# Masking moved from TensorE to GpSimd, set-up waits split, and a new written order in a one-core two-layer kernel

## The chip, the cores and the metric

The kernel runs on one core of one Trainium2 chip. Five engines each run their own instruction stream, in order, and meet only at semaphores: TensorE (PE; its weight loads are listed as PEld), VectorE (DVE), ScalarE (ACT), GpSimd (POOL) and SyncE (SP), which issues nearly all DMAs. The metric is the time of the device in microseconds. The kernel before took 343.66 us (median of 3 runs, 339.81 to 346.64).

## The reference, cut to what matters

There are two sequences (B = 2) of 512 rows of 128 features. Three stages follow each other:

```
x = x + ffn0(softmax-scaled x)            # ternary weights, rounded activations: gate, up, down (128 -> 512 -> 128)
c = causal_attention(x, image)            # 16 heads of width 8; key 0 is one image key, keys 1.. are words
                                          # scores = where(kj <= qi + 1, q.k / sqrt(8), -10000) + mask; softmax; @ v; project
y = layernorm(c + full_attention(c))      # 16 heads again, no mask
y = layernorm(y + experts(y))             # 8 experts 128 -> 256 -> 128, one chosen per row
x = x + y
```

The products of queries and keys must be exact to float32, so each is held as three bfloat16 parts that are stacked along the contraction.

## The kernel before, in words

**Instances.** There are four attentions, `a` = 0 to 3: 0 and 1 are the causal one of either sequence, 2 and 3 the full one. Each has 64 `scores` steps (16 heads by 4 tiles of 128 queries; TensorE L1308 into a PSUM bank, VectorE takes the row maximum, L1025 for a < 2 and L1029 for a >= 2) and 32 `attend` steps. An `attend` step works on one head and two blocks of 128 keys: TensorE recomputes the scores turned round with the maximum already taken off (L1331), ScalarE takes the exponent into `probs` (L800, float32), and `values` steps multiply by the values (L1349). Four heads share one accumulation in `ps_pv`.

**The causal mask.** For a < 2 the blocks to the right of the diagonal are not computed. In the 128x128 block on the diagonal a future key has to count nothing: after each L1331 a second matmul (L1334) adds a triangle of -1e30 (`causal_k` by `identb`) before the exponent. There are 2 for each of 64 `attend` steps, 128 in all. The row maximum has its own triangle, added by L1025 on VectorE; the change leaves that alone.

**Set-up and the first stage.** SP loads all inputs (L478 to L508) and then copies zeroed rows three times (L511, 1 MB each). ScalarE sums the absolute weights (L689), scales them (L699); VectorE rounds weights (`ternary`, L842/L843) and x (`rounded_x`, L833/L836). For sequence a: `ffn_in` turns the rounded x; `ffn_up` (four tiles) is two matmuls (L1244), a Silu (L740), a product (L959) and a maximum (L962) on VectorE, and after the fourth tile a chain of small VectorE steps that ends in `q2_ready` (L972). `r2t` scales on ScalarE (L747, `Y`), rounds on VectorE (L976, `R2`) and turns on TensorE (L1253); `down` copies that from PSUM on VectorE (L979, `R2T`) and multiplies (L1262). `x1` adds the residual on VectorE (L986); `x1t` turns it (L1270), ScalarE copies (L755). `q` and `k` are one matmul each (L1284, L1288), ScalarE writes them in float32 (L763, L769) and then the high bfloat16 part (L766, L772). Steps `q_parts` and `k_parts` on VectorE make the rest (L993, L1000), the middle part (L994, L1001, a cast) and the low part (L996, L1003). `send` on SP writes the parts to DRAM (L544, L550) and loads them back stacked (L472); `scores` of that instance wait for these loads, and those of instance 0 also for `fixed_rows`, 12 small DMAs on SP (L521 to L526). `turn_weights` (TensorE L1195 to L1202, ScalarE L715 to L732), `prepare` (VectorE L928 to L943 with a small TensorE step, L1206 to L1209) and `images` (TensorE L1214 to L1228, ScalarE L751, VectorE L948 to L954) are set-up that the later stages need. The memsets of `Vs` (GpSimd, L624) come in the steps `stacks`.

**The order.** No planner runs in the kernel. The string `MERGE` is a written-out order: each letter takes the next step of a chain, every engine walks the same list and issues its own part of each step. So a step that stands earlier in the list on an engine holds up all that stands behind it there. In the old list the start reads, by steps: setup, ffn_in.0, turn_down, round_x, ffn_up.0[0-2], ffn_in.1, ffn_up.0[3], turn_weights, ffn_up.1[0], the r2t and down steps of sequence 0, prepare, x1.0, ffn_up.1[1-2], x1t.0, ffn_up.1[3], q.0, q_parts.0, k.0, k_parts.0, images, the r2t and down steps of sequence 1, scores.0[0-4], x1.1, scores.0[5-8], fixed_rows, more scores.0, send.0. The second instance's q_parts stands behind scores.0[49], its k_parts behind scores.0[53], and the first attend step behind scores.0[51].

**The end.** The experts (`hidden` L1424, `y` L1437, both TensorE in float32) follow the last attention; then a layer norm with small VectorE and GpSimd steps, and the output DMAs.

## Time and profile before

| what | value |
|---|---|
| runs of the kernel before | 343.66 us median of 3 (339.81 to 346.64) |
| the profiled execution, its own time | 341.08 us |
| its span, first to last instruction | 339.3 us |
| TensorE, matmul records | 294.3 us, 87% |
| VectorE | 256.6 us, 76% |
| ScalarE | 170.0 us, 50% |
| GpSimd | 28.6 us, 8% |
| mean granted TensorE clock | 0.943 |

A matmul's record runs from its start to its modelled end, and the next one may start long before that; so TensorE's busy time is an upper bound of the time for which it can take no further matmul. Two starts in a row tell what a matmul takes of the stream. The chain of waits follows the execution back from its last instruction. A granted clock of 1.0 is 2.4 GHz, of 0.5 is 1.2 GHz.

### The profile page before, as it was taken

How to read it: one execution, taken by the hardware profiler on the slowest of the kernel's cores; microseconds unless marked ns; L12 is line 12 of the kernel's file. 1: busy time of each engine (PE TensorE's matmuls, PEld its weight loads, DVE VectorE, ACT ScalarE, POOL GpSimd, SP SyncE). 2: the span in 40 equal slices, each digit the busy share in tenths (PEclk: the TensorE clock that was granted, in tenths of full speed). 3: DMA queues.
4: the chain of work that ended last, by engine and by line, in shares of the span. 5: the costliest groups of instructions: out<-in, count | busy, mean ns of one | idle time of the engine just before them, and what ended most of it. 6: DMA issues, size and time to landing. Idle time of an engine off the chain costs nothing.

```text
span 339.3 us, 5440 instructions
## 1 busy us (share of the span) xinstructions
PE 294.3 (87%) x1888; PEld 149.5 (44%) x1888; DVE 256.6 (76%) x764; ACT 170.0 (50%) x246; POOL 28.6 (8%) x58
## 2 busy tenths in 40 slices
PE   0286874988899999999999999999999999999990
PEld 0134351335544544454433332334444357776770
DVE  5887976999778779999899988887932134665765
ACT  1865540046465666474486756763868721221210
POOL 3061000005060000000000000002100000000101
PEclk9996765599999999999999999999999999999997
DMA  7793157203554006540015440080000000000011
GB/s 174 176 212 74 27 174 177 59 3 122 144 97 81 4 8 193 125 92 2 2 38 177 103 101 0 3 248 2 0 2 2 0 2 0 1 2 0 2 31 32
DMA packets 14991, 22.83 MB, mean 67 GB/s; under 512 B 2222, under 2 KB 12338, under 8 KB 14196
## 3 DMA queue, kind: packets, MB, share of 16 engines
q1 hardware_dynamic: 14676, 22.21, 26.5%
q0 software_dynamic: 288, 0.28, 0.7%
q8 instruction: 15, 0.25, 0.3%
q14 instruction: 12, 0.10, 0.1%
HBM read 13.99 MB, written 4.72 MB: 55 GB/s over the span
## 4 chain that ended last, share of the span: by engine, by line
PE 54%; DVE 15%; issue 11%; DMA 8%; SPq 8%; ACT 2%; POOLq 0%; POOL 0%; DVEq 0%; ACTq 0%
PE ps_pv L1349 14%; PE ps_s L1308 11%; PE ps_t L1331 9%; DVE mx L1029 7%; PE ps_s L1424 6%; PE ps_misc L1437 5%; DMA Ks<-Qs 5%; DVE shared L1025 2%; SPq L521 2%; SPq L508 2%; DVE mx L1025 1%; ACT probs L800 1%; SPq L544 1%; PE ps_t L1334 1%; DMA Ks<-parts_k 1%
## 5 line engine op out<-in xcount | busy, mean ns | idle before, releaser
L800 ACT ACTIVATE probs<-ps_t 128x1024 f32<-128x1024 f32 (+2 forms) x128 | 106.1, 861 | 58.8 <-PE ps_t L1334 27.8
L1029 DVE TENSOR_REDUCE mx<-ps_s 128x1 f32<-128x512 f32 x128 | 81.9, 685 | 10.4 <-PE ps_s L1308 9.9
L1308 PE MATMUL ps_s<-Ks,Qs 128*128 128x512 bf16 (+2 forms) x235 | 75.9, 353 | 10.0 <-DVE mx L1025 3.4
L1331 PE MATMUL ps_t<-Qs,Ks 128*128 128x512 bf16 (+3 forms) x256 | 67.6, 340 | 0.9 <-ACT probs L800 0.7
L1349 PE MATMUL ps_pv<-probs,Vs 128*32 128x512 f32 (+3 forms) x512 | 55.9, 523 | 0.0
L1025 DVE CUSTOM_DVE_ANT_0 shared<-ps_s,shared 128x256 bf16<-128x256 f32 (+3 forms) x107 | 46.4, 461 | 12.3 <-PE ps_s L1308 11.9
L1308 PEld LDWEIGHTS ps_s<-Ks,Qs 128*128 128x128 bf16 x235 | 21.9, 98 | 65.9 <-DVE mx L1029 31.0
L1331 PEld LDWEIGHTS ps_t<-Qs,Ks 128*128 128x128 bf16 x256 | 24.0, 98 | 24.3 <-issue 5.9
L786 ACT ACTIVATE shared<-ps_s,cols 128x512 f32<-128x512 f32 x16 | 11.0, 686 | 40.4 <-PE ps_s L1424 40.4
L1137 DVE SCALAR_TENSOR_TENSOR shared<-ps_misc,comb,shared 128x128 f32<-128x128 f32 x48 | 13.5, 343 | 23.0 <-PE ps_misc L1437 23.0
L1424 PE MATMUL ps_s<-Qf,Ks 128*128 128x512 f32 x64 | 30.4, 597 | 0.0
L1437 PEld LDWEIGHTS ps_misc<-Ks,shared 128*128 128x128 f32 x192 | 23.0, 192 | 4.0 <-issue 3.7
L1334 PE MATMUL ps_t<-causal_k,identb 128*128 128x128 bf16 x128 | 24.6, 219 | 0.0
L1437 PE MATMUL ps_misc<-Ks,shared 128*128 128x128 f32 x192 | 23.5, 275 | 0.1
L669 POOL TENSOR_TENSOR shared<-shared,halves 128x4 f32<-128x4 f32 x4 | 4.1, 1035 | 187.4 <-DVE shared L851 187.4
L1349 PEld LDWEIGHTS ps_pv<-probs,Vs 128*32 128x32 f32 x512 | 11.2, 108 | 18.6 <-issue 16.9
L1124 DVE TENSOR_SCALAR shared<-ps_s,cols 128x512 f32<-128x512 f32 x16 | 11.9, 746 | 8.5 <-PE ps_s L1424 8.4
L1424 PEld LDWEIGHTS ps_s<-Qf,Ks 128*128 128x128 f32 x64 | 11.1, 190 | 8.9 <-issue 8.2
L1334 PEld LDWEIGHTS ps_t<-causal_k,identb 128*128 128x128 bf16 x128 | 12.5, 98 | 3.3
L783 ACT ACTIVATE shared<-ps_pv 128x512 f32<-128x512 f32 x16 | 9.5, 595 | 7.8 <-PE ps_pv L1349 7.8
L1025 DVE CUSTOM_DVE_ANT_0 shared<-ps_t,shared 128x512 bf16<-128x512 f32 (+1 forms) x21 | 12.3, 623 | 0.0
L1308 PE MATMUL ps_t<-Ks,Qs 128*128 128x512 bf16 (+1 forms) x21 | 10.0, 498 | 1.7 <-DVE mx L1025 0.7
(263 smaller groups left out, 330.6 us busy)
## 6 DMA issues: line engine op xcount, KB each, us to landing
parts_q<-Qp SPq DMA_DIRECT2D x20, 128.0 KB, 1.9
Qs<-parts_q SPq DMA_DIRECT2D x24, 96.0 KB
Ks<-parts_k SPq DMA_DIRECT2D x24, 96.0 KB
Qs<-parts_q SPq DMA_DIRECT2D x12, 192.0 KB
Ks<-parts_k SPq DMA_DIRECT2D x12, 192.0 KB
Ks<-Qs SPq DMA_DIRECT2D x2, 1024.0 KB, 12.1
parts_k<-Kp SPq DMA_DIRECT2D x12, 128.0 KB, 1.8
Qs<-Qs SPq DMA_DIRECT2D x1, 1024.0 KB, 12.1
```

Of the source, the lines that this page charges most:

```text
L786: act.activation(hid[:, i % 2, 1, :], ps[:, :], ACT.Relu, bias=cols17[:, 2 * i + 1:2 * i + 2])\
L800: act.activation(probs[:, half % 2, j, 0:w], ps[:, 0:w], ACT.Exp).then_inc(free[f"t{i % 2}"], 1)
L1025: last = dve.tensor_tensor_reduce(out=added[:, n % 2, 0:w], in0=ps[:, 0:w], in1=causal_q[:, S - w:], scale=1.0, scalar=LEAST, op0=ALU.add, ...
L1029: last = dve.tensor_reduce(mx[:, b, t, h:h + 1], ps[:, 0:w], AX, ALU.max)
L1124: dve.tensor_scalar(hid[:, i % 2, 0, :], ps[:, :], cols17[:, 2 * i:2 * i + 1], 0.0, ALU.add, ALU.max).then_inc(free["s0"], 1)
L1137: last = dve.scalar_tensor_tensor(out=acc[:, a, t, :], in0=rows, scalar=comb[:, a, t, i // 2, i % 2:i % 2 + 1], in1=acc[:, a, t, :], op0=A ...
L1308: mm = pe.matmul(ps[:, 0:w], Qs[:, b, h, t * P:(t + 1) * P], Ks[:, b, h, 0:w], start=True, stop=True)
L1331: mm = pe.matmul(ps[:, col:col + w], Ks[:, b, h, kb * P:(kb + 1) * P], Qs[:, b, h, S - w:S], start=True, stop=(a >= 2))
L1334: mm = pe.matmul(ps[:, col:col + P], identb[:, :], causal_k[:, :], start=False, stop=True)
L1349: mm = pe.matmul(ps[j * HC:(j + 1) * HC, S - w:S], Vs[:, b, kb, r * GROUP + j, :], probs[:, half % 2, j, col:col + w], start=(kb == 0), st ...
L1424: pe.matmul(ps[:, :], W1[:, i, h * P:(h + 1) * P], X3T[:, a, :], start=True, stop=True)\
L1437: mm = pe.matmul(rows, hid[:, i % 2, h, t * P:(t + 1) * P], W2[:, i, h, :], start=(h == 0), stop=(h == FH - 1))
```

## The change

1. The 128 triangle matmuls L1334 and their tile `causal_k` go. Instead GpSimd, in every `attend` step of a < 2, waits for the exponent and sets the future half of the two diagonal blocks in `probs` to zero with one `affine_select` of 128x256 float32. `values` wait for a count of these (`future_zeroed`) where they waited for the exponents.
2. Set-up waits are split: ScalarE waits for each of the three weights alone; the maximum of x, its scale and rounding are done by sequence (`scale_of_x`, `scale_of_products`), the second sequence's in `round_x`; `x1t` turns each tile of x1 as it is made; one small VectorE step of the `q2` chain is folded into another.
3. The high parts of q and k are taken by ScalarE from PSUM; the middle parts are cast by ScalarE (`q_mid`, `k_mid`) in place of VectorE. The rounding and the PSUM copy of `r2t` and `down` go to ScalarE for sequence 1.
4. `q_parts` and `k_parts` become six steps, and `MERGE` is new. Its start reads: setup, ffn_in.0, turn_down, turn_weights, round_x, ffn_up.0[0-1], ffn_in.1, prepare, ffn_up.0[2-3], the r2t and down steps of sequence 0, x1.0, stacks.0, ffn_up.1[0-1], x1t.0, q.0, q_res.0, ffn_up.1[2], k.0, q_mid.0, k_res.0, images, ffn_up.1[3], r2t.1[0-1], k_mid.0, down.1[0], r2t.1[2], down.1[1], r2t.1[3], down.1[2-3], q_lo.0, fixed_rows, stacks.1, k_lo.0, load_small, x1.1, scores.0[0-20], send.0. Later q_res.1 stands behind scores.0[45], k_lo.1 behind scores.0[52], the first attend step behind scores.0[47]. Between the last attend step of a half and its values stand, for a < 2, at least 4 scores or attend steps in the new list, at least 2 in the old.

```diff
 for a in range(INST):
     chains["0123"[a]] = each("scores", a, HEADS * NT)
-    chains["4567"[a]] = [(n, a, 0) for n in ("q_parts", "k_parts", "send", "late")]
+    chains["4567"[a]] = [(n, a, 0) for n in ("q_res", "q_mid", "k_res", "k_mid", "q_lo", "k_lo", "send", "late")]
...
-in_x, in_w3, in_att, in_mask, in_moe = (sem(n) for n in
-                                        ("in_x", "in_w3", "in_att", "in_mask", "in_moe"))
+in_x, in_att, in_mask, in_moe = (sem(n) for n in ("in_x", "in_att", "in_mask", "in_moe"))
+in_w3 = [sem(f"in_w3_{n}") for n in range(3)]
...
-sp.wait_ge(qhi_ready, a + 1)
+sp.wait_ge(free["misc"], filled("misc", "q", a))
...
-sp.wait_ge(khi_ready, a + 1)
+sp.wait_ge(free["misc"], filled("misc", "k", a))
...
+if step == "attend" and a < 2:
+    r, u, j = unit(i)
+    half = 2 * (a * ROUNDS + r) + u
+    pool.wait_ge(free[f"t{i % 2}"], filled(f"t{i % 2}", "weights", a, i))
+    (_, _, w), _ = blocks_of(a, u)
+    early_two = probs[:, half % 2, j, 0:2 * w].rearrange("p (k q) -> p k q", k=2)[:, :, 0:P]
+    pool.affine_select(out=early_two, in_=early_two, compare_op=ALU.is_ge, fill=0.0, base=0,
+                       pattern=[[0, 2], [1, P]], channel_multiplier=-1).then_inc(future_zeroed, 1)
...
-act.wait_ge(in_w3, 16 * 3)
 for n in range(3):
+    act.wait_ge(in_w3[n], 16)
...
-act.wait_ge(scale_ready, 1)
+act.wait_ge(scale_ready, a + 1)
...
+    if a == 1:
+        two_ago = divmod(t - 2, NT)
+        act.wait_ge(full[f"t{i % 2}"], filled(f"t{i % 2}", "r2t", *two_ago))
+        act.wait_ge(y_ready, t + 1)
+        act.activation(R2[:, t % 2, :], Y(i), ACT.Identity, bias=unmagic[:, 0:1]).then_inc(r2_ready, 1)
+if step == "down" and a == 1:
+    ps = take(f"t{i % 2}", "r2t", a, i)
+    act.activation(R2T[:, i % 2, :], ps[:, 0:INNER // 2].bitcast(bf16), ACT.Copy)\
+       .then_inc(free[f"t{i % 2}"], 1)
...
     act.activation(Qf[:, b, :], ps[:, :], ACT.Identity, bias=cols5[:, 0:1] if a < 2 else bjoin[:, 0:1],
+                   scale=float(HD) ** -0.5)
+    act.activation(Qp[:, 0, :], ps[:, :], ACT.Identity,
+                   bias=cols5[:, 0:1] if a < 2 else bjoin[:, 0:1],
                    scale=float(HD) ** -0.5).then_inc(free["misc"], 1)
-    act.wait_ge(free["misc"], filled("misc", "q", a))
-    act.activation(Qp[:, 0, :], Qf[:, b, :], ACT.Copy).then_inc(qhi_ready, 1)
 if step == "k":
     ps = take("misc", "k", a)
     act.activation(Kf[:, :], ps[:, :], ACT.Identity,
+                   bias=cols5[:, 1:2] if a < 2 else bjoin[:, 1:2])
+    act.activation(Kp[:, 0, :], ps[:, :], ACT.Identity,
                    bias=cols5[:, 1:2] if a < 2 else bjoin[:, 1:2]).then_inc(free["misc"], 1)
-    act.wait_ge(free["misc"], filled("misc", "k", a))
-    act.activation(Kp[:, 0, :], Kf[:, :], ACT.Copy).then_inc(khi_ready, 1)
+if step == "q_mid":
+    act.wait_ge(qres_ready, a + 1)
+    act.activation(Qp[:, 1, :], qres[:, :], ACT.Copy).then_inc(qrest_ready, 1)
+if step == "k_mid":
+    act.wait_ge(kres_ready, a + 1)
+    act.activation(Kp[:, 1, :], kres[:, :], ACT.Copy).then_inc(krest_ready, 1)
...
+def scale_of_x(n):
+    r = slice(n * NT, (n + 1) * NT)
+    then_wait(dve.tensor_tensor(q1[:, 0, r], q1[:, 0, r], wdot[:, 0, r], ALU.mult))
+    then_wait(dve.tensor_scalar(q1[:, 0, r], q1[:, 0, r], 1e-5, None, ALU.max))
+    then_wait(dve.reciprocal(q1[:, 1, r], q1[:, 0, r]))
+    then_wait(dve.tensor_scalar(q1[:, 1, r], q1[:, 1, r], 127.0, None, ALU.mult))
+def scale_of_products(n):
+    r = slice(n * NT, (n + 1) * NT)
+    then_wait(dve.tensor_scalar(q1[:, 2, r], q1[:, 0, r], 1.0 / 127.0, None, ALU.mult))
+    dve.tensor_scalar(q1[:, 4, r], q1[:, 2, r], wmean[:, 1:2], None, ALU.mult)
+    dve.tensor_scalar(q1[:, 3, r], q1[:, 2, r], wmean[:, 0:1], None, ALU.mult).then_inc(scale_ready, 1)
...
-dve.tensor_reduce(q1[:, 0, :], X[:, :, :], AX, ALU.max, apply_absolute_value=True)
+dve.tensor_reduce(q1[:, 0, 0:NT], X[:, 0:NT, :], AX, ALU.max, apply_absolute_value=True)
...
-    then_wait(dve.tensor_tensor(q1[:, 0, :], q1[:, 0, :], wdot[:, 0, :], ALU.mult))
-    then_wait(dve.tensor_scalar(q1[:, 0, :], q1[:, 0, :], 1e-5, None, ALU.max))
-    then_wait(dve.reciprocal(q1[:, 1, :], q1[:, 0, :]))
-    then_wait(dve.tensor_scalar(q1[:, 1, :], q1[:, 1, :], 127.0, None, ALU.mult))
+    scale_of_x(0)
     ternary(0)
     ternary(1)
     rounded_x(0)
-    then_wait(dve.tensor_scalar(q1[:, 2, :], q1[:, 0, :], 1.0 / 127.0, None, ALU.mult))
-    dve.tensor_scalar(q1[:, 4, :], q1[:, 2, :], wmean[:, 1:2], None, ALU.mult)
-    dve.tensor_scalar(q1[:, 3, :], q1[:, 2, :], wmean[:, 0:1], None, ALU.mult).then_inc(scale_ready, 1)
+    scale_of_products(0)
 if step == "round_x":
+    then_wait(dve.tensor_reduce(q1[:, 0, NT:], X[:, NT:, :], AX, ALU.max, apply_absolute_value=True))
+    scale_of_x(1)
     rounded_x(1)
+    scale_of_products(1)
...
-        dve.tensor_scalar(q2[:, 3, r], q2[:, 0, r], wmean[:, 2:3], 1.0 / 127.0, ALU.mult, ALU.mult)
-        then_wait(dve.tensor_scalar(q2[:, 1, r], q2[:, 1, r], 127.0, None, ALU.mult))
-        dve.tensor_tensor(q2[:, 2, r], q2[:, 1, r], q1[:, 4, r], ALU.mult).then_inc(q2_ready, 1)
-if step == "r2t":
-    t = a * NT + i
+        then_wait(dve.scalar_tensor_tensor(out=q2[:, 2, r], in0=q2[:, 1, r], scalar=127.0,
+                                           in1=q1[:, 4, r], op0=ALU.mult, op1=ALU.mult))
+        dve.tensor_scalar(q2[:, 3, r], q2[:, 0, r], wmean[:, 2:3], 1.0 / 127.0, ALU.mult, ALU.mult)\
+           .then_inc(q2_ready, 1)
+if step == "r2t" and a == 0:
+    t = i
     dve.wait_ge(y_ready, t + 1)
     dve.tensor_scalar(R2[:, t % 2, :], Y(i), MAGIC, None, ALU.subtract).then_inc(r2_ready, 1)
-if step == "down":
+if step == "down" and a == 0:
...
+        if t < NT - 1:
+            last.then_inc(x1_tiles, 1)
     last.then_inc(free["pv"], 1)
-if step == "q_parts":
-    dve.wait_ge(qhi_ready, a + 1)
-    then_wait(dve.tensor_tensor(qres[:, :], Qf[:, b, :], Qp[:, 0, :], ALU.subtract))
-    dve.tensor_copy(Qp[:, 1, :], qres[:, :]).then_inc(qrest_ready, 1)
+if step == "q_res":
+    dve.wait_ge(free["misc"], filled("misc", "q", a))
+    dve.tensor_tensor(qres[:, :], Qf[:, b, :], Qp[:, 0, :], ALU.subtract).then_inc(qres_ready, 1)
+if step == "k_res":
+    dve.wait_ge(free["misc"], filled("misc", "k", a))
+    dve.tensor_tensor(kres[:, :], Kf[:, :], Kp[:, 0, :], ALU.subtract).then_inc(kres_ready, 1)
+if step == "q_lo":
     dve.wait_ge(qrest_ready, a * (PARTS - 1) + 1)
     dve.tensor_tensor(Qp[:, 2, :], qres[:, :], Qp[:, 1, :], ALU.subtract).then_inc(qrest_ready, 1)
-if step == "k_parts":
-    dve.wait_ge(khi_ready, a + 1)
-    then_wait(dve.tensor_tensor(kres[:, :], Kf[:, :], Kp[:, 0, :], ALU.subtract))
-    dve.tensor_copy(Kp[:, 1, :], kres[:, :]).then_inc(krest_ready, 1)
+if step == "k_lo":
     dve.wait_ge(krest_ready, a * (PARTS - 1) + 1)
     dve.tensor_tensor(Kp[:, 2, :], kres[:, :], Kp[:, 1, :], ALU.subtract).then_inc(krest_ready, 1)
...
-pe.wait_ge(free["pv"], filled("pv", "down", a))
 ps = put("misc", "x1t", a)
 for t in range(NT):
+    if t < NT - 1:
+        pe.wait_ge(x1_tiles, a * (NT - 1) + t + 1)
+    else:
+        pe.wait_ge(free["pv"], filled("pv", "down", a))
     mm = pe.transpose(ps[:, t * P:(t + 1) * P], X1[:, a * NT + t, :], ident[:, :])
...
     mm = pe.matmul(ps[:, col:col + w], Ks[:, b, h, kb * P:(kb + 1) * P],
-                   Qs[:, b, h, S - w:S], start=True, stop=(a >= 2))
-    if a < 2:
-        mm = pe.matmul(ps[:, col:col + P], identb[:, :], causal_k[:, :],
-                       start=False, stop=True)
+                   Qs[:, b, h, S - w:S], start=True, stop=True)
 mm.then_inc(full[f"t{i % 2}"], 1)
...
+if i == 0:
+    pe.wait_ge(free["misc"], filled("misc", "v", a))
 ps = put("pv", "values", a, r) if kb == 0 else place["pv"]
 if kb % 2 == 0:
     for n in (2 * GROUP * r + GROUP * u + 2, 2 * GROUP * r + GROUP * u + 3):
-        pe.wait_ge(free[f"t{n % 2}"], filled(f"t{n % 2}", "weights", a, n))
+        if a >= 2:
+            pe.wait_ge(free[f"t{n % 2}"], filled(f"t{n % 2}", "weights", a, n))
+    if a < 2:
+        pe.wait_ge(future_zeroed, (half + 1) * GROUP)
```

## Rows read from the trace of the kernel before

**Rows 1.** The page: the chain of waits, shares of the span by engine and line.

```profile
PE 54%; DVE 15%; issue 11%; DMA 8%; SPq 8%; ACT 2%; POOLq 0%; POOL 0%; DVEq 0%; ACTq 0%
PE ps_pv L1349 14%; PE ps_s L1308 11%; PE ps_t L1331 9%; DVE mx L1029 7%; PE ps_s L1424 6%; PE ps_misc L1437 5%; DMA Ks<-Qs 5%; DVE shared L1025 2%; SPq L521 2%; SPq L508 2%; DVE mx L1025 1%; ACT probs L800 1%; SPq L544 1%; PE ps_t L1334 1%; DMA Ks<-parts_k 1%
```

**Rows 2.** Windows: stretch, length, busy PE, PEld, DVE, ACT, POOL, then clock, DMA.

```profile
80.00:110.00 30.00, 28.38 (x259) 14.75 (x259) 24.78 (x105) 16.95 (x27) 7.03 (x13) 1.00 0.49 114
...
140.00:170.00 30.00, 29.07 (x234) 13.51 (x234) 27.91 (x52) 15.78 (x27) 0.68 (x1) 1.00 0.18 42
...
290.00:320.00 30.00, 30.00 (x182) 22.40 (x182) 18.87 (x69) 6.31 (x11) 0.81 (x1) 1.00 0.00 1
```

**Rows 3.** Timeline of SP: start, length, line, what, count (no compute, only issues).

```profile
40.17 0.73 SPq L526 DMA_DIRECT2D Qs<-orow  x1
41.00 4.64 SPq L544 DMA_DIRECT2D parts_q<-Qp  x5
45.68 1.51 SPq L550 DMA_DIRECT2D parts_k<-Kp  x3
...
49.40 1.18 SPq L472 DMA_DIRECT2D Ks<-parts_k  x3
```

**Rows 4.** Timeline of VectorE: the first maximum of `scores`, and instance 1's parts.

```profile
53.84 0.29 DVE L1025 CUSTOM_DVE_ANT_0 shared<-ps_s,shared 128x128 bf16<-128x128 f32 x1 [3.70 <-PE ps_s L1308]
...
77.66 1.26 DVE L994 CAST Qp<-qres 128x512 bf16<-128x512 f32 x1
...
82.52 0.43 DVE L1001 CAST Kp<-kres 128x512 bf16<-128x512 f32 x1
82.98 0.69 DVE L1003 TENSOR_TENSOR Kp<-kres,Kp 128x512 bf16<-128x512 f32 x1
```

**Rows 5.** Timeline of ScalarE in set-up.

```profile
9.12 0.63 ACT L689 ACTIVATE probs<-shared 128x512 f32<-128x512 f32 x1 [7.10 <-DMA shared<-in_L_ffn_w_down]
...
24.41 0.45 ACT L715 ACTIVATE WinT<-ps_misc 128x128 f32<-128x128 f32 x2 [0.23 <-PE ps_misc L1195]
...
25.44 0.19 ACT L724 ACTIVATE condT<-ps_t 128x2 f32<-128x2 f32 x1
...
40.18 0.63 ACT L766 ACTIVATE Qp<-Qf 128x512 bf16<-128x512 f32 x1
...
45.34 2.92 ACT L747 ACTIVATE probs<-probs,magic,q 128x512 f32<-128x512 f32 x4
```

**Rows 6.** Timeline of VectorE in set-up.

```profile
20.37 0.69 DVE L959 TENSOR_TENSOR probs<-probs,ps_t 128x512 f32<-128x512 f32 x1 [0.86 <-ACT probs L740]
...
27.12 0.16 DVE L972 TENSOR_TENSOR q<-q 128x4 f32<-128x4 f32 x1
...
32.40 0.25 DVE L928 COPY rows5p<-rows 5x128 f32<-5x128 f32 x1
...
35.09 1.12 DVE L986 SCALAR_TENSOR_TENSOR X<-ps_pv,q,X 128x128 f32<-128x128 f32 x4
```

**Rows 7.** Timeline of TensorE in set-up: up matmuls of sequence 1, first and last of `images`.

```profile
33.84 1.87 PE L1244 MATMUL ps_t<-shared 128*128 128x512 bf16 x4
...
41.16 0.39 PE L1214 MATMUL ps_s<-WsqT,condT 128*128 128x128 f32 x2
...
44.02 0.89 PE L1228 MATMUL ps_s<-WinT,WcpT 128*128 128x384 f32 x2
```

**Rows 8.** Timeline of TensorE in the causal stage: a triangle and what follows it.

```profile
97.18 0.22 PE L1334 MATMUL ps_t<-causal_k,identb 128*128 128x128 bf16 x1
97.23 0.38 PE L1308 MATMUL ps_s<-Ks,Qs 128*128 128x512 bf16 x1
```

**Rows 9.** Timeline of GpSimd: a selection, a long memset, a product of two inputs.

```profile
2.45 0.34 POOL L610 TENSOR_SCALAR_AFFINE_SELECT head_grid<-head_grid 128x128 f32<-128x128 f32 x1
...
76.72 1.92 POOL L624 MEMSET Vs<- 128x512 f32 x4
...
94.47 0.69 POOL L663 TENSOR_TENSOR Zimg<-Vimg,Pimg 128x288 f32<-128x288 f32 x1 [13.30 <-ACT Pimg L780]
```

30 lines of the change are left out of this document (15 added, 15 removed).

## The prediction

> **What bounds the kernel now.** I read the chain of waits first [rows 1]: 54% of the span is TensorE, 15% VectorE, and another 16% are DMAs and SP's issues, nearly all of them before the first `scores`. So there are three stages. *Set-up* ends when VectorE takes the first maximum at 53.84 [rows 4]. What it waits for is SP's row: the last of the fixed rows is issued at 40.17, the parts of q from 41.00, those of k until 47.19, the loads back from 49.40 [rows 3]; ScalarE had the high part of q at 40.81 [rows 5], just in time. *The middle* runs from there to about 245. The windows [rows 2] show two engines near their limit: in 80 to 110 TensorE has records over 28.4 of 30 us and VectorE over 24.8; in 140 to 170 VectorE is at 27.9 of 30, the tighter of the two. TensorE's figure overstates, since a record overlaps the next. *The end*, experts in float32, has TensorE busy for 30.00 of 30 us [rows 2]; what is gained before it counts if TensorE reaches it sooner.
>
> **Set-up, step by step.** Times are of the profiled execution.
> - Split wait for the weights: two of three sums (0.63 each) now precede the landing at 9.12 [rows 5]; about 1.1 us earlier.
> - `turn_weights` now stands ahead of the first `ffn_up`. ScalarE's copies from 24.41 to 25.63 [rows 5] must free a PSUM place first, and I allow 0.9 us for TensorE's transposes. They were hidden beside VectorE's products; here nothing covers them. First product: 20.37 [rows 6] - 1.1 + 1.2 + 0.9 = about 21.4.
> - `prepare` now stands between tiles 1 and 2. It took 32.40 to 35.09, 2.7 us [rows 6], with TensorE's small matmuls inside. Behind it TensorE must still do tile 2's matmuls and ScalarE its Silu, before VectorE has a product again. Two products and two maxima (4 x 0.69 [rows 6]) end at 24.1; the small matmuls, the up matmuls and the Silu I put at 2.7 more; four more steps and the small chain (about 1.0) end at 30.5. That is where 27.28 stood: 3.2 later.
> - Behind `down` the 2.7 us of `prepare` are gone; not all of that is won, as `Y` and `R2` start without the backlog that hid ScalarE. `x1` starts at 35.09 + 3.2 - 2.1 = 36.2.
> - TensorE then has four up matmuls (1.87 [rows 7]) ahead of `x1t`; they ran beside `prepare` before. All tiles of x1 are ready when they end, so the split wait of `x1t` gives nothing. In the old trace the high part of q is complete 4.6 us after x1; now 37.7 + 4.4 = 42.1, 1.3 later than before, and SP is free at 40.9, so nothing else holds it.
> - k follows on TensorE until 43.0, then `images`: 41.16 to 44.91, 3.75 us [rows 7], to 46.8. Then tile 3's matmul and Silu (1.3), product and maximum (1.4), chain (1.0): 50.4. VectorE has all that ahead of `q_lo`: 51.1.
> - `k_mid` stands behind two tiles of `Y` and `R2`. `Y` takes 0.73 [rows 5]; `R2` on ScalarE is not in the trace: at least the 0.43 of a cast on VectorE [rows 4], at most the 0.73 of `Y`, same shape and engine; I take 0.7. 50.4 + 2.9 + 0.6 = 53.9, and `k_lo` (0.69 [rows 4]) ends at 54.7.
> - SP: last part of k issued by 55.3, landed 2 us after its issue, loads from 56.8. From these loads to the first maximum it was 49.40 to 53.84, 4.4 us [rows 3, 4]: **61.2, or 7.3 us later**. Bounds: +4, if TensorE's small matmuls in `prepare` and `images` cost little; +9, if `images` runs at the lower clock. `x1.1` (1.1 us) falls into this wait.
>
> **The middle.**
> - From the first maximum to the end of instance 1's low part of k it was 53.84 to 83.67, 29.8 us [rows 4], all VectorE. Gone from it: x1.1 (1.1), both casts (1.26 + 0.43 [rows 4]), and one tile of `scores` (0.4), as the step stands one earlier. **-3.2**. The same casts on ScalarE (0.63 each [rows 5]) are covered: it is busy 17 of 30 us [rows 2].
> - Triangles: one takes 97.18 to 97.23, 0.055 us of TensorE's stream [rows 8]; its record of 0.22 is mostly latency that the next matmul overlaps. 128 x 0.055 = 7.1 us. The chain passes over 1% of the span, 3.4 us of them [rows 1]. The first is the upper end; 3.4 is a middle value, and nothing the lower end, where VectorE holds TensorE anyway in the stretch from 140 [rows 2]. I take **-5.3**, the mean of 3.4 and 7.1, since most triangles lie before 140, where VectorE has 5 of 30 us free.
> - Casts of instances 2 and 3: 4 x 0.43 [rows 4] of an engine at 93%. **-1.0**; between 0 and -1.7.
> - GpSimd's zeroing, 64 times on 256 columns: at least the 0.34 of a selection of 128, at most the 0.69 of a product over 288 [rows 9]; I take 0.5, 32 us of an engine that is idle. It lies between exponent and values. At least 4 `scores` or `attend` steps stand there in the new list, and a step costs VectorE 0.3 to 0.7 us, so it is covered: 0. Without the cover it is a rival below.
> - GpSimd's memsets and small loads move to where it is idle: 0. Waits on it: `Zimg` queues with the zeroing in the same order as ScalarE works: 0.
> - New order of the rest: 0, between -4 and +3; the list has the same steps and the trace does not price it.
>
> **A rule against it.** The cast of 77.66 took 1.26 us while GpSimd's memsets ran from 76.72, and 0.43 at 82.52 with GpSimd idle [rows 4, 9]. By the Trainium skill ("SBUF — State Buffer", on the shared port pair) GpSimd and VectorE hold that pair exclusively, and a VectorE instruction with two SBUF inputs waits for a GpSimd instruction that reads SBUF, as the zeroing does. By that rule the casts gain by leaving, and some 16 two-input steps of VectorE (residuals, low parts, normalising) could each wait up to 0.5 us; the sum would be up to 8 us less good if every one met a zeroing.
>
> **Sum.** +7.3 - 3.2 - 5.3 - 1.0 = -2.2: the profiled execution's 341.08 would be 338.9. It stands 2.6 below the median of the runs, so against 343.66 I give 341.5.
>
> **The rivals.**
> - *The middle gives back more.* In 80 to 110 both engines have slack [rows 2], so waits between them are worth something, and the end is bound by TensorE alone. With the start only 3 us later, all 7.1 of the triangles, 3.2 and 1.7 of casts, and 1 from the order: -10, 333.7. Against it: the start would have to be better than my steps. Chance 0.30.
> - *The low part of k decides (slower).* Place: VectorE's wait before its first maximum. Start 9 later, less 1.1 for x1.1, and in the middle VectorE holds the pace, so that triangles become waits of TensorE for a maximum: +7.9, 351.6. It decides if the middle gives less than the start loses, 7.3. For it: VectorE at 93% in 140 to 170 [rows 2]. Against: the casts leave just that engine. Chance 0.15.
> - *Zeroing stands in the way.* If values wait for it at each of 16 halves, 16 x 0.5 = 8.0: -2.2 + 8.0 = +5.8, 349.5. Against: the distance in the list. The rule above would give the same size by another path. Chance 0.05.
> - *The change does nothing that counts*: the DMAs hold the start where it was, TensorE the rest. It lies inside the forecast's range.
>
> **How the numbers follow.** Forecast 0.50, its own range 336 to 347 from the bounds of start (+4 to +9) and triangles. 2% of 343.66 is 6.9 us, about what a measurement tells from no change: below 336.8 is faster, above 350.5 slower. Most of the first rival and the low tail of the forecast: 0.30. Two thirds of the second and the tails: 0.16. Within: 0.54. The range for 8 in 10 takes in most of the first rival and ends at the second: 331.5 to 350.5.
>
> **What would show it.** Right: first maximum near 61; q_lo late on VectorE behind the product of tile 3; no L1334 records and TensorE's busy time some 25 us less, with its stream only 7 less; casts gone from VectorE; zeroing of about 0.5 each. Wrong: a first maximum before 57; values that wait for GpSimd for over 3 us in total; VectorE idle for over 8 of 30 us in the middle; or an end stage that is longer, which no step here touches.

## The result and the profile after

The changed kernel takes 343.33 us (median of 20 runs, 341.86 to 346.18); beside it the kernel before took 342.4 (20 runs). The ratio is **1.0054, 95% interval 1.0032 to 1.0077**: slower by 1.8 us, where 2.2 us faster was forecast. All ratios here are taken from fast runs alone (a run over 1.5% above the fastest of its kernel counts as slow, one of 558.6 us in e18 among them), so they are not the ratios of the medians. The two spans below differ by 1.2 us. The profiled execution took 342.62 us, its span is 340.5; before it was 341.08 and 339.3.

The page's chain of waits after, to be read against [rows 1]:

```profile
PE 54%; DVE 22%; issue 16%; ACT 5%; DMA 1%; POOLq 0%; POOL 0%; SPq 0%; DVEq 0%; ACTq 0%
PE ps_pv L1391 13%; PE ps_t L1371 10%; PE ps_s L1348 10%; DVE mx L1066 8%; PE ps_s L1466 4%; PE ps_misc L1479 4%; DVE shared L1062 3%; DVE mx L1062 1%; DMA X<-in_x 1%; ACT probs L755 1%; DVE probs L995 1%; PE ps_misc L1324 1%; PE ps_misc L1328 1%; PE ps_misc L1354 1%; PE ps_t L1281 1%
```

DMAs and SP have all but left the chain (16% before, 1% now), and VectorE stands at 22% where it had 15. "issue" has risen from 11 to 16%: that is time for which the profile shows no releaser, and the scores' wait for loaded parts, twice below, is booked there, so part of the DMAs' share may have changed its name only. The windows of [rows 2], after:

```profile
80.00:110.00 30.00, 27.09 (x199) 12.60 (x198) 27.00 (x109) 20.43 (x33) 10.22 (x24) 1.00 0.43 116
140.00:170.00 30.00, 26.66 (x196) 9.96 (x195) 28.59 (x56) 14.72 (x25) 9.57 (x21) 1.00 0.26 58
290.00:320.00 30.00, 29.68 (x172) 21.32 (x171) 22.53 (x81) 6.18 (x11) 1.91 (x2) 1.00 0.03 10
```

In these stretches TensorE is less busy and VectorE more: 27.0 and 28.6 of 30 us, against 24.8 and 27.9. But the changed kernel runs 3 to 5 us late there, so the same clock times hold other work. Between two points of the same work, the low parts of k of instances 1 and 2 (K1 and K2 of the table below), VectorE is busy for as long as before and TensorE for 2.1 us less. Before, then after:

```profile
83.67:131.40 47.73, 45.35 (x397) 22.84 (x389) 38.45 (x161) 28.79 (x49) 6.60 (x11) 1.00 0.35 81
88.28:134.35 46.07, 43.22 (x341) 19.51 (x342) 38.01 (x158) 30.69 (x53) 16.49 (x39) 1.00 0.29 75
```

The end stage is nearly full as before.

The rows that answer to [rows 3 to 6]. SP:

```profile
42.04 9.37 SPq L546 DMA_DIRECT2D parts_q<-Qp  x5
51.46 3.78 SPq L552 DMA_DIRECT2D parts_k<-Kp  x3
55.29 1.21 SPq L474 DMA_DIRECT2D Qs<-parts_q  x3
```

VectorE, from the first product of set-up to the low part of k of instance 1 (its cast on this engine is gone):

```profile
21.61 0.69 DVE L995 TENSOR_TENSOR probs<-probs,ps_t 128x512 f32<-128x512 f32 x1 [1.14 <-ACT probs L748]
...
50.25 0.23 DVE L1008 TENSOR_SCALAR q<-q,wmean 128x4 f32<-128x4 f32 x1
50.38 0.69 DVE L1037 TENSOR_TENSOR Qp<-qres,Qp 128x512 bf16<-128x512 f32 x1
54.20 0.69 DVE L1040 TENSOR_TENSOR Kp<-kres,Kp 128x512 bf16<-128x512 f32 x1 [3.14 <-ACT Kp L796]
60.17 1.13 DVE L1023 SCALAR_TENSOR_TENSOR X<-ps_pv,q,X 128x128 f32<-128x128 f32 x4 [5.27 <-PE ps_pv L1299]
61.21 0.28 DVE L1062 CUSTOM_DVE_ANT_0 shared<-ps_s,shared 128x128 bf16<-128x128 f32 x1
...
87.60 0.68 DVE L1040 TENSOR_TENSOR Kp<-kres,Kp 128x512 bf16<-128x512 f32 x1
```

ScalarE and TensorE in front of the first maximum:

```profile
50.51 0.81 ACT L755 ACTIVATE probs<-probs,magic,q 128x512 f32<-128x512 f32 x1 [2.62 <-DVE q L1008]
51.41 0.72 ACT L761 ACTIVATE shared<-probs,unmagic 128x512 bf16<-128x512 f32 x1
...
53.56 0.61 ACT L796 ACTIVATE Kp<-kres 128x512 bf16<-128x512 f32 x1
54.08 0.57 ACT L764 ACTIVATE R2T<-ps_t 128x512 bf16<-128x512 bf16 x1
...
58.87 0.60 ACT L764 ACTIVATE R2T<-ps_t 128x512 bf16<-128x512 bf16 x1 [0.22 <-PE ps_t L1290]
```

```profile
59.52 0.61 PE L1299 MATMUL ps_pv<-shared,R2T 128*128 128x128 bf16 x4 [0.21 <-ACT R2T L764]
60.67 0.48 PE L1348 MATMUL ps_s<-Ks,Qs 128*128 128x128 bf16 x2 [0.55 <-issue]
```

The first score comes 0.55 us after a `down` product that waited for ScalarE; the profile names no releaser for these 0.55, and the loads of the parts are what the program waits for there. So two paths end together here: the parts of k, and `Y`, `R2`, `R2T` of instance 1, which now share one engine and take 9.0 us for four tiles (50.51 to 59.47). The chain of waits runs over the second.

The group of the zeroing, and one of the weight loads of `scores`:

```profile
L672 POOL TENSOR_SCALAR_AFFINE_SELECT probs<-probs 128x256 f32<-128x256 f32 x64 | 26.2, 414 | 50.2 <-ACT probs L824 50.0
L1348 PEld LDWEIGHTS ps_s<-Ks,Qs 128*128 128x128 bf16 x230 | 21.4, 97 | 63.9 <-DVE mx L1066 32.9 <-DVE mx L1062 16.5 <-issue 7.9
```

**Milestones**, read from each timeline (us). M1 is the start of the first causal maximum; K1, K2, K3 the end of the low part of k of instances 1, 2, 3; F the first full maximum (instance 2); L the end of the last one. The names of the other kernels follow below.

| kernel | M1 | K1 | K2 | F | K3 | L | span |
|---|---|---|---|---|---|---|---|
| before | 53.84 | 83.67 | 131.40 | 137.80 | 181.77 | 244.89 | 339.3 |
| changed | 61.21 | 88.28 | 134.35 | 141.25 | 184.13 | 247.02 | 340.5 |
| e1 early low parts | 54.68 | 86.09 | 132.19 | 139.21 | 182.09 | 244.96 | 338.5 |
| e2 old set-up order | 55.56 | 85.30 | 131.37 | 139.51 | 183.46 | 246.33 | 339.8 |
| e4 before + zeroing | 53.04 | 83.99 | 137.96 | 145.06 | 189.59 | 252.73 | 347.1 |
| e10 the same, loads early | 54.08 | 84.07 | 132.23 | 140.15 | 184.65 | 247.78 | 342.2 |
| e5 triangles back | 60.99 | 87.79 | 136.06 | 143.03 | 185.62 | 248.51 | 342.0 |
| e7 half full maxima | 60.93 | 87.92 | 134.01 | 141.06 | 180.26 | 241.70 | 335.5 |
| e8 e7 + triangles | 60.84 | 87.76 | 136.03 | 143.01 | 183.76 | 245.26 | 339.1 |
| e11 all maxima half | 61.33 | 84.45 | 129.21 | 136.01 | 176.82 | 238.24 | 332.0 |
| e12 e11 + triangles | 61.98 | 86.36 | 133.35 | 140.26 | 181.00 | 242.42 | 336.2 |
| e9 casts on VectorE | 64.30 | 91.65 | 137.84 | 144.59 | 189.30 | 252.18 | 345.7 |
| e17 e2 + R2 casts back | 53.48 | 81.86 | 128.13 | 136.06 | 180.14 | 243.38 | 336.9 |

From before to changed: the start loses 7.37, M1 to K1 gives back 2.76, K1 to K2 1.66, K2 to L 0.82 and the end 0.93. That leaves 1.2 us of span. The 0.93 at the end go with the new list: from L on, the kernels with the old one (before, e4, e10) take 94.4 us, the changed kernel, e1 and e2 93.5. What in it does that stays open.

Two things to keep in mind with this table. The profiled execution of e2 took 341.91 us where the median of its runs is 340.04. And the granted clock of TensorE between 140 and 150 is 0.83 in e2, e4, e9 and e10 and 1.00 in before, changed, e1 and e5; in e17 it is 0.83 from 130 to 140. Ten microseconds at 0.83 hold 1.7 us less of full clock, an estimate from these rows, so of K2 to K3 only kernels with the same clock can be compared.

### The profile page after: what moved, and what is told of

The parts are those of the page before. It is cut to its first block, busy times and chain, and to the rows that moved or that the text cites. A ratio compares the mean times of both kernels' runs of the same rounds, so it can differ in the third digit from the quotient of the medians.

```text
span 340.5 us, 5253 instructions
## 1 busy us (share of the span) xinstructions
PE 286.8 (84%) x1760; PEld 140.5 (41%) x1760; DVE 252.2 (74%) x754; ACT 178.2 (52%) x262; POOL 54.7 (16%) x121
## 4 chain that ended last, share of the span: by engine, by line
PE 54%; DVE 22%; issue 16%; ACT 5%; DMA 1%; POOLq 0%; POOL 0%; SPq 0%; DVEq 0%; ACTq 0%
PE ps_pv L1391 13%; PE ps_t L1371 10%; PE ps_s L1348 10%; DVE mx L1066 8%; PE ps_s L1466 4%; PE ps_misc L1479 4%; DVE shared L1062 3%; DVE mx L1062 1%; DMA X<-in_x 1%; ACT probs L755 1%; DVE probs L995 1%; PE ps_misc L1324 1%; PE ps_misc L1328 1%; PE ps_misc L1354 1%; PE ps_t L1281 1%
## 5 line engine op out<-in xcount | busy, mean ns | idle before, releaser
L1066 DVE TENSOR_REDUCE mx<-ps_s 128x1 f32<-128x512 f32 x124 | 79.6, 686 | 10.2 <-PE ps_s L1348 9.8
L1348 PE MATMUL ps_s<-Ks,Qs 128*128 128x512 bf16 (+2 forms) x230 | 73.8, 350 | 8.3 <-DVE mx L1062 3.3
L1371 PE MATMUL ps_t<-Qs,Ks 128*128 128x512 bf16 (+3 forms) x256 | 62.7, 340 | 0.6 <-DMA Qs<-nmT 0.4
L1062 DVE CUSTOM_DVE_ANT_0 shared<-ps_s,shared 128x128 bf16<-128x128 f32 (+1 forms) x106 | 46.0, 460 | 7.5 <-PE ps_s L1348 6.4
L1348 PEld LDWEIGHTS ps_s<-Ks,Qs 128*128 128x128 bf16 x230 | 21.4, 97 | 63.9 <-DVE mx L1066 32.9
L672 POOL TENSOR_SCALAR_AFFINE_SELECT probs<-probs 128x256 f32<-128x256 f32 x64 | 26.2, 414 | 50.2 <-ACT probs L824 50.0
L1371 PEld LDWEIGHTS ps_t<-Qs,Ks 128*128 128x128 bf16 x256 | 22.6, 99 | 26.7 <-issue 9.2
L1290 PE MATMUL ps_t<-identb,shared 128*128 128x128 bf16 x32 | 4.9, 309 | 13.1 <-ACT shared L761 7.7
L1348 PE MATMUL ps_t<-Ks,Qs 128*128 128x512 bf16 (+1 forms) x26 | 11.7, 485 | 1.4 <-DVE mx L1062 0.2
L1062 DVE CUSTOM_DVE_ANT_0 shared<-ps_t,shared 128x384 bf16<-128x384 f32 (+1 forms) x22 | 12.8, 620 | 0.0
```

The lines of the kernel that those rows point to most:

```text
L672: pool.affine_select(out=early_two, in_=early_two, compare_op=ALU.is_ge, fill=0.0, base=0, pattern=[[0, 2], [1, P]], channel_multiplier=-1 ...
L1062: last = dve.tensor_tensor_reduce(out=added[:, n % 2, 0:w], in0=ps[:, 0:w], in1=causal_q[:, S - w:], scale=1.0, scalar=LEAST, op0=ALU.add, ...
L1066: last = dve.tensor_reduce(mx[:, b, t, h:h + 1], ps[:, 0:w], AX, ALU.max)
L1348: mm = pe.matmul(ps[:, 0:w], Qs[:, b, h, t * P:(t + 1) * P], Ks[:, b, h, 0:w], start=True, stop=True)
L1371: mm = pe.matmul(ps[:, col:col + w], Ks[:, b, h, kb * P:(kb + 1) * P], Qs[:, b, h, S - w:S], start=True, stop=True)
```

## Experiments

All ratios are to the kernel before, run beside it.

**Does the late start reach the end?** e1 takes the low parts ahead of `images` and spreads r2t and down of instance 1 among the scores; e2 has the old set-up order. Only the start of the list differs:

```diff
-ffwwTffgwffffffffffuSggff4gf44Uggg4gggggg4VS4Sv00000000000
+ffwwTffgwffffffffffuSggff4gf44444UgggVSS00g0000g0g0000g0g00g000v     (e1)
+ffwTfffgfwgffffffffwuSggfgf4f44444UggggggggVSS0000v                   (e2)
```

> The changed kernel with another list at the start: the steps 4 (k_mid, q_lo, k_lo) right behind k_res, ahead of the images and of the second instance's r2t and down steps, and those spread between the first 0 steps, as before the change. Theory A (what the start loses reaches the end): the first causal maximum ends near 54 us in place of 61.2, and most of the 7.3 us stays, so 336 to 338 us. Theory B (VectorE's column of work of the middle sets the end and the start's gap is filled later, because the same r2t, down and x1 work still has to be done on VectorE and ScalarE): the first maximum is earlier by 7, but k_lo of the second instance and the maxima of the middle move by 2 or less, so 341 to 343 us.

> The changed kernel with the old order of the set-up up to the first score (the weights turned one column of the list later, the quantisation of the second instance back in its place, the low parts ahead of the images), and the new list behind it; the steps of the second instance stay ahead of the scores. Theory A: the first maximum comes between 54 and 59 us and the end moves by as much, 337 to 341 us. Theory B (what the second instance's feed-forward needs before its own q and k is what counts): the first maximum is earlier, k_lo of the second instance isn't, and the time stays 342 to 344 us.

Measured: e1 340.78 us, 0.9983 (0.9953 to 1.0013); e2 340.04 us, 0.9968 (0.9936 to 1.0001). e1 puts the first maximum 6.5 us earlier and gains 2.2 at K1 and 2.0 at the end. So a third of these 6.5 us reaches the end; the other two thirds are used up between M1 and K1 (31.4 us in e1, 27.1 in the changed kernel), where e1 does the r2t and down steps of instance 1 that the changed kernel has done by then. e1 falls between its two theories and nearer to B. e2's time is theory A's, but e2 is 5.7 us ahead at M1 and 3.0 at K2, so it too loses half on the way; by the ratios it is 0.86%, 2.9 us, ahead of the changed kernel. From K2 to F it loses another 1.2, and from F to K3, at the lower clock, 1.1. In its chain of waits TensorE stands in front of the first full score, whose parts are being loaded:

```profile
136.28 0.79 PE ps_misc L1354 x8
137.07 2.03 issue
139.10 0.38 PE ps_s L1348
```

**What is the zeroing worth in the old list?** e4 is the kernel before with part 1 of the change alone, e3 all changed code in the old list.

```diff
-                        if a < 2:
-                            mm = pe.matmul(ps[:, col:col + P], identb[:, :], causal_k[:, :], ...)
+                if step == "attend" and a < 2:      # on GpSimd, as in the change
+                    pool.affine_select(out=early_two, in_=early_two, compare_op=ALU.is_ge, fill=0.0, ...)
```

> The kernel before with one part of the change alone: the triangle products of the weights are gone, GpSimd zeroes the future probabilities, everything else and the list as before. On record the triangles were put at 5.3 us on the path. If TensorE's stream is the bound where they stood: 337 us (342.4 less 5.3). If VectorE's maxima and ScalarE's exponentials hold the middle: 340 to 341.5 us. If the extra hop over GpSimd (0.41 us for one, and the wait for it) stands on the path in a list that leaves it no room: 342.5 us or more.

> All instructions of the changed kernel in the order of the kernel before (its list, with its 4 to 7 steps split into the eight new ones in the same places). If the new list of the middle costs what the rest of the change gained, this is 5 us or more faster than the kernel before: 336 to 338 us. If the triangles are worth only 2 to 3 us because VectorE's maxima hold the middle, it gains those 2 to 3 us and the late x1 order's nothing: 339 to 341 us. If the zeroing on GpSimd holds the values back, it is no faster than the kernel before.

Measured: e4 347.08 us, 1.0170 (1.0124 to 1.0215); e3 351.72 us, 1.0303 (1.0263 to 1.0343). Both are in the branch in which the zeroing holds the values back, further out than any number that I had named. GpSimd's timeline in e4:

```profile
106.48 0.78 POOL L640 DMA_DIRECT2D Wr<-in_L_ffn_w_group  x1
...
111.23 0.54 POOL L640 DMA_DIRECT2D norm_gb<-in_L_ffn_ln_b  x1
111.77 0.78 POOL L674 TENSOR_SCALAR_AFFINE_SELECT probs<-probs 128x256 f32<-128x256 f32 x2
```

and TensorE's:

```profile
108.90 0.28 PE L1318 MATMUL ps_s<-Ks,Qs 128*128 128x256 bf16 x1 [0.20 <-DVE mx L1035]
112.25 1.08 PE L1361 MATMUL ps_pv<-probs,Vs 128*32 128x256 f32 x8 [3.07 <-POOL probs L674]
```

and the windows:

```profile
100.00:110.00 10.00, 8.23 (x66) 3.34 (x65) 8.56 (x38) 6.23 (x10) 6.30 (x14) 1.00 0.37 69
110.00:120.00 10.00, 7.75 (x40) 3.95 (x41) 3.29 (x15) 2.99 (x6) 3.72 (x9) 0.56 0.24 28
```

Nine small loads stand in a row on GpSimd's queue, 5.3 us of issuing. One zeroing is behind them, the values behind it, the scores behind these; and in the ten microseconds of the standstill and after it TensorE's granted clock is 0.56, mostly its lower level of 1.2 GHz. In the kernel before the same loads (95.10 to 100.39) cost nothing, as nobody waited for that queue. The changed kernel has them at 31.00.

e10 is e4 with these loads at the set-up; e15 is e3 with the same edit:

```diff
-        "S": [("stacks", 0, 0), ("stacks", 1, 0), ("load_small", 0, 0)],
+        "S": [("load_small", 0, 0), ("stacks", 0, 0), ("stacks", 1, 0)],     # first S right behind u
```

> As the run of the kernel before with the zeroing alone (347.08 us, 5.5 above before), but GpSimd's nine small loads (5.3 us of issuing in a row on its queue, at 106.5 there) stand at the set-up, as in the changed kernel. In that run one zeroing waited behind them, TensorE stood for 3.1 us and its granted clock fell to 0.56 in the next 10. If this queue was the whole loss, the zeroing now gives what the triangles are worth: 339 to 341 us, 2 below before. If the hop itself costs in the old list, 344 us or more.

> All instructions of the changed kernel in the old list, but with GpSimd's nine small loads in the set-up. The changed code in the plain old list took 351.72 us; the kernel before with the zeroing lost 4.9 us of its span by these loads. If they are the whole fault of the old list, this is 343 to 344 us, as the changed kernel is. If the rest of the new list is worth something of its own, it stays at 346 to 348.

Measured: e10 342.74 us, 1.0036 (0.9999 to 1.0072); e15 345.27 us, 1.0084 (1.0044 to 1.0124). In e10 the window is whole again:

```profile
110.00:120.00 10.00, 9.19 (x79) 4.30 (x75) 7.33 (x33) 5.42 (x10) 3.83 (x9) 1.00 0.02 4
```

The queue cost 1.3% in e4 and 2.2% in e3, 4.6 and 7.5 us. e10 and e15 came out between their branches (339 to 341 or 344 and more; 343 to 344 or 346 to 348). Without these loads in front of it, the zeroing in the old list is worth nothing: K1 to K2 takes 48.2 us in e10 and 47.7 before, K1 to F 56.1 and 54.1. It isn't the hop over GpSimd that takes the gain back: for zeroings TensorE's weight loads wait 0.6 us in all of e10. What has grown from K1 to K2 is their wait for VectorE's causal maxima. Before, and in e10 (us in total, times, longest):

```profile
PEld ps_s L1308 <- DVE mx L1025: 7.5, 17, 0.8
PEld ps_s L1318 <- DVE mx L1035: 12.5, 26, 0.8
```

So in the old list TensorE without its triangles has less to do there, and waits for VectorE longer. Between K2 and F it loses another 1.5 us; of its wait in front of the first full score 1.8 us have no releaser in the profile, so where these go stays open.

The new list as a whole is worth 0.3%, 1 us, against e15 (1.0054 and 1.0084), with intervals that leave room from nothing to over 2 us. That small sum hides two larger parts. e2, which has nearly e15's set-up order and the new list behind it, stands at 0.9968: so the new list behind the set-up is worth some 1.2%, 4 us, and the new order of the set-up costs 0.86%, 2.9 us.

**What are the triangles worth in the new list, and does VectorE cover them?** e5 is the changed kernel with the triangles back; e6 makes each zeroing twice; e7 and e8 are a pair with the full maxima halved, e11 and e12 a pair with all maxima halved (the maximum then leaves out half of the scores).

```diff
-                    last = dve.tensor_reduce(mx[:, b, t, h:h + 1], ps[:, 0:w], AX, ALU.max)
+                    last = dve.tensor_reduce(mx[:, b, t, h:h + 1], ps[:, 0:w // 2], AX, ALU.max)      (e7, e8, e11, e12)
-    ...tensor_tensor_reduce(out=added[:, n % 2, 0:w], in0=ps[:, 0:w], in1=causal_q[:, S - w:], ...)
+    ...tensor_tensor_reduce(out=added[:, n % 2, 0:w // 2], in0=ps[:, 0:w // 2], in1=causal_q[:, S - w:S - w // 2], ...)   (e11, e12)
+    then_wait(pool.affine_select(out=early_two, in_=early_two, ...))      # once more, ahead of the other (e6)
```

> The changed kernel, its new list kept, with the triangle products back on TensorE and no zeroing on GpSimd. On record the triangles were put at 5.3 us; by that this is 5.3 us slower than the changed kernel, 348.5 us. If VectorE's maxima hold the middle and cover most of them, it is 1 to 3 us slower. If the zeroing's hop over GpSimd costs what the triangles cost, it is the same within 1 us or faster. The old list lost 5.8 us by the zeroing, so the wait for GpSimd is real; whether this list hides it is what this run and the next tell.

> The changed kernel with each zeroing on GpSimd made twice, the second behind the first (0.41 us and a semaphore more before the values are released, 64 times). If the new list hides the hop, the time is the changed kernel's within 1 us. If the values wait for GpSimd as in the old list, it costs up to 64 x 0.5 = 32 us at most, and 5 us or more where one in five of them is on the path.

> The changed kernel with the 128 full maxima of the later instances taken over 256 of their 512 columns (half of the scores is left out of the maximum; everything else, the list too, is as it is). It relieves VectorE by about 128 x 0.3 = 38 us where the waits name it most. If VectorE's maxima hold the middle, 10 to 25 us faster than the changed kernel. If TensorE's stream holds it, 3 us or less.

> As e7, with the triangle products back on TensorE and no zeroing. The pair gives the worth of the triangles where VectorE has time to spare: if VectorE covered them, they cost 4 to 7 us here against 1 to 3 in the pair with full maxima; if the pair shows the same difference as the other, VectorE wasn't what covered them.

> The changed kernel with all 256 maxima over half of their columns, the causal ones too (half of the scores is left out of them). With the full maxima alone halved it gained 4 us, all of it behind 134 us. If VectorE's causal maxima pace the middle before that too, the stretch from the low part of k of instance 1 to that of instance 2 (46.07 us in the changed kernel) becomes 43 or less; if TensorE's own stream is what fills it, it stays at 45 to 46.

> As e11 with the triangles back and no zeroing. If VectorE hid the rest of the triangles (7.1 us of stream, of which the pair with full maxima shows 2.2 in that stretch and 0 behind it, and the pair with the full ones halved 2.2 and 1.5), the difference of this pair is 5 to 7 us. If it is 2 to 4 again, the triangles' stream was overstated: a triangle of 0.055 us then fits into gaps that TensorE has for other reasons, the wait for ScalarE's exponentials among them.

Measured: e5 344.81 us, 1.0110 (1.0068 to 1.0152), so the triangles' removal, with the zeroing that replaces it, is worth 0.56% or **1.9 us** in this list (1.5 in the spans); that is in the 1 to 3 us of the branch in which VectorE's maxima cover most. e6 344.49, 1.0094 (1.0063 to 1.0126): the second zeroing costs 1.4 us. TensorE's weight loads wait for GpSimd in five places there, 3.4 us, and in the changed kernel in one, 0.4 us. So the new list hides most of the hop, not all. e7 339.56, 0.9939 (0.9899 to 0.9979); e8 341.46, 0.9998 (0.9969 to 1.0027); e11 334.0, 0.9795 (0.9745 to 0.9845); e12 337.99, 0.9879 (0.9814 to 0.9945).

e7 is 3.9 us faster than the changed kernel, between its branches of "3 or less" and "10 to 25", and e11 needs 44.76 us from K1 to K2, between "43 or less" and "45 to 46". The pairs differ by 2.0 us (e7, e8) and 2.9 (e11, e12), which is the branch by which it isn't VectorE's load that covers the triangles. The runs alone don't tell the pairs apart (0.56%, 0.59%, 0.84%), and single intervals are as wide as the differences. The milestones say more. The triangles' records in e5 and their count between the milestones (10 start before K1, 72 between K1 and K2, 46 behind K2):

```profile
L1369 PE MATMUL ps_t<-causal_k,identb 128*128 128x128 bf16 x128 | 24.3, 219 | 0.0
```

Between K1 and K2, 72 x 0.055 = 4.0 us of stream cost 2.2 us with full maxima (48.27 against 46.07) and 2.2 with all halved (46.99, 44.76). The pair with only the full ones halved repeats the first here (48.27, 46.09), since the full maxima come behind K2. So the other half isn't covered by how busy VectorE is: in the third pair it has 10 us less to do in this stretch. It is still a wait for VectorE that grows when the triangles go: the weight loads of `scores` wait for a causal maximum for 8.4 us in e5 and 9.7 in the changed kernel, and for 4.9 in e12 and 6.0 in e11; the time without a releaser grows by about as much again. That reads as gaps that each score has for the maximum before it, whatever its length, but no run takes these gaps away, so it is not shown. Behind K2, 46 x 0.055 = 2.5 us of stream cost nothing until L with full maxima (e5 is 1.7 later at K2 and 1.5 at L), and 1.5 us with halved ones (2.0 later at K2, 3.6 at L). There VectorE is the cover. In the third pair they cost nothing behind K2 either, which doesn't fit; but e11's granted clock is 0.84 from 130 to 140 where e12's is 1.00, about 1.6 us of full clock by the estimate above, which may hide it.

**What are the casts worth?** e9 is the changed kernel with all four casts back on VectorE; e17 and e18 are e2 with two of them back each.

```diff
-                if step == "r2t" and a == 0:          # VectorE; the ScalarE copy for a == 1 goes   (e9, e17)
+                if step == "r2t":
-                if step == "down" and a == 0:
+                if step == "down":
-                    act.activation(Qp[:, 1, :], qres[:, :], ACT.Copy)        # likewise Kp          (e9, e18)
+                    dve.tensor_copy(Qp[:, 1, :], qres[:, :])
```

> The changed kernel, its list kept, with the four kinds of casts back on VectorE (R2, R2T of instance 1, the middle parts of q and k). On record their move was put at 1.3 + 0.4 us in the middle and 1.0 later, together some 3 us. If that holds, this is 3 us slower than the changed kernel (1.4% above the kernel before). If the start's low part of k waited for ScalarE (k_mid behind Y and R2), part of it comes back and the first maximum is 1 to 2 us earlier than 61.2: then the time is within 1 us of the changed kernel's.

> The changed kernel with the old set-up order (its second run stood at 340.04 us), and R2 and R2T of instance 1 cast on VectorE again; the middle parts stay on ScalarE. All four kinds together were worth 5.2 us of span in the changed list, 3.1 of them before the first maximum. If that came from the second instance's R2 and R2T in front of the low parts, nothing of it is left where the low parts stand first: then 340 to 341 us here. If VectorE's time as such counts, 4 x (0.43 + 0.43) = 3.4 us slower, 343.5.

> As the run before, but R2 and R2T on ScalarE and the middle parts of q and k of all instances cast on VectorE. In the set-up it saves a hop between two engines, so the first maximum may come 0.5 us earlier than 55.6. From then on VectorE has 6 x 0.43 = 2.6 us more to do, 0.9 before the last causal maximum and 1.7 in front of the loads of instances 2 and 3: 341 to 342.5 us if VectorE holds them, 340 if not.

Measured: e9 347.56 us, 1.0188 (1.0139 to 1.0237); e17 **337.86 us, 0.9896 (0.9856 to 0.9935)**; e18 344.52 us, 1.0060 (1.0023 to 1.0096). In the changed list the four casts on ScalarE are worth 1.3%, 4.6 us, more than the 3 forecast, and M1 came 3.1 us later in place of 1 to 2 earlier, since VectorE has k's middle and low parts queued behind R2 and R2T there (K of instance 0 ends at 57.07 in e9, at 54.89 in the changed kernel). Where the low parts stand first, ScalarE is the wrong place for R2 and R2T: e17 is 0.72%, 2.5 us, ahead of e2, where I had expected nothing or a loss. For the middle parts it is the right one: e18, with them on VectorE, is 0.92%, 3.1 us, behind e2, more than the 1 to 2.5 forecast. e18 is level with e2 at K1 and K2 (85.22 and 131.43) and loses 2.2 us from K2 to K3, where four of these casts (1.7 us) are; its clock between 140 and 150 is 0.73 where e2 has 0.83. e2's timeline of ScalarE:

```profile
46.32 0.80 ACT L755 ACTIVATE probs<-probs,magic,q 128x512 f32<-128x512 f32 x1
...
53.36 0.58 ACT L764 ACTIVATE R2T<-ps_t 128x512 bf16<-128x512 bf16 x1
```

and e17's, `Y` on ScalarE beside the last copy on VectorE:

```profile
46.09 2.92 ACT L755 ACTIVATE probs<-probs,magic,q 128x512 f32<-128x512 f32 x4
...
50.47 0.42 DVE L1007 COPY R2T<-ps_t 128x512 bf16<-128x512 bf16 x1 [0.43 <-PE ps_t L1281]
```

The last copies start 2.9 us apart. TensorE meets the first scores behind the last `down` in its stream, and in these two executions its clock comes back earlier:

```profile
50.00:60.00 10.00, 7.04 (x37) 3.18 (x35) 4.19 (x19) 4.35 (x7) 0.00 (x0) 0.50 0.77 162
60.00:70.00 10.00, 9.12 (x30) 3.66 (x29) 10.00 (x49) 0.60 (x1) 0.00 (x0) 0.50 0.21 42
70.00:80.00 10.00, 8.43 (x31) 3.82 (x31) 8.09 (x37) 4.53 (x8) 0.68 (x1) 0.74 0.05 15
```

for e2, and for e17:

```profile
50.00:60.00 10.00, 6.66 (x29) 2.42 (x26) 6.89 (x33) 0.00 (x0) 0.00 (x0) 0.67 0.73 182
60.00:70.00 10.00, 8.57 (x33) 3.98 (x33) 9.24 (x45) 0.60 (x1) 0.00 (x0) 0.59 0.16 39
70.00:80.00 10.00, 7.95 (x42) 4.09 (x43) 10.00 (x40) 7.71 (x12) 1.36 (x3) 1.00 0.17 56
```

e17 is 3.4 us ahead of e2 at K1 and 2.9 at the end. How much of this is the clock and how much the earlier scores isn't told apart. It beats both kernels: zeroing on GpSimd, small loads early, middle parts on ScalarE, R2 and R2T on VectorE, the old set-up order.

**Can the transfer in front of the first full score be had?** The steps of q and k of instance 2 moved up in the list: all nine by four places (e13 on e2, e14 on e1), or the last five by two (e19 on e2).

```diff
-B1aBI11aBB11q11b6B116q11bBB666q1161B1     (e1, e2)
+B1aBI11aqBB11611b6qB111616b6BqB6111B1     (e13, e14)
+B1aBI11aBB11q11b6B116q11b6B6B6q6111B1     (e19)
```

> The changed kernel with the old set-up order (as in the second run of the first four) and the nine steps of q and k of instance 2 four places earlier in the list. There TensorE stood for 2.03 us at 137.07, in front of the first full score of instance 2, because its parts were still on their way. If the parts' path sets that start, the gap closes and 1 to 2 us of the end with it: 338 to 339 us against 342.4 before. If TensorE's and VectorE's work behind it is what counts, the time stays at 340.

> As the run before, on the start with the early low parts (first run of the first four), where the gap in front of that score was 0.91 us: 0 to 1 us faster than that run's 340.8.

> The changed kernel with the old set-up order and only the last steps (k_res, k_mid, q_lo, v, k_lo) of instance 2 two places earlier. Moving all nine steps by four made TensorE wait elsewhere (1.1 us at 126.44, before values) and gained nothing. If two places are within the slack, the wait of 2.03 us before the first full score shrinks to under 1.2 and the time to 339 us; if the steps' place is tied to VectorE's maxima, it is 340 or more again.

Measured: e13 343.0 us, 1.0030 (0.9997 to 1.0063); e14 344.41, 1.0079 (1.0044 to 1.0113); e19 340.64, 0.9974 (0.9945 to 1.0002). A miss for the first two, which even lose: e13 0.6% (2 us) to e2, e14 1.0% (3 us) to e1. In e13 the wait only shrinks:

```profile
139.19 1.30 issue
```

and K2, meant to come earlier, ends at 132.53 where e2 has 131.37: TensorE now waits elsewhere, 1.1 us at 126.44 for a zeroing on GpSimd, and the same 1.1 in e14. Here the hop does stand in the way, in a list that was only moved elsewhere; a run with the values later wasn't made. e19 ends K2 at 130.15 and F at 138.59, 0.9 us before e2, and its span is 0.8 shorter; in the runs it can't be told from e2.

## Why the prediction was wrong

**The set-up was right** as a number: first maximum forecast at 61.2, measured 61.21. Along the way: first product 21.4 and 21.61; the q2 chain's end 30.5 and 31.13; x1 36.2 and 36.68; the high part of q 42.1 and 41.97; q_lo 51.1 and 51.07; k_lo 54.7 and 54.89. One thing it didn't see: a second path, instance 1's casts on ScalarE, ends within 0.55 us of the first score. In e2, where the low part of k ends 10 us earlier, that path holds M1: from the first load of parts to M1 it takes 8.6 us, against 5.9 in the changed kernel and 5.3 in e17, which has these casts on VectorE. And the 7.3 us weren't a price that the end pays in full, as e1 and e2 show (6.5 and 5.7 earlier, 2 to 3 us of time).

**The middle** (-3.2) gave 2.8 between M1 and K1. Right as a number, but the reasons are not all borne out: 1.7 of it was to come from both casts leaving VectorE, and e9, with both back on VectorE, takes 27.35 us there against 27.07. Of the old cast of 1.26 us, 0.83 had gone anyway: in e9 it takes 0.43, since the memsets are no longer beside it.

**Triangles (-5.3): this step failed.** They gave 1.9 us (e5), 1.5 in the span, net of the zeroing, which held TensorE up for 0.4. I had taken the mean of the chain's 3.4 and the full stream of 7.1 for what the path gets back. The 0.055 us of stream each was right, and so was nothing behind K2, where VectorE holds. But between K1 and K2 as well only 2.2 of 4.0 us came back: with less to stream, TensorE waits longer for causal maxima. "VectorE has 5 of 30 us free" was no ground for counting on the stream: free time on VectorE doesn't keep TensorE from waiting for the next maximum. The result lay below the chain's share, which was itself a rounded 1%. All I expected behind K1 was -6.3, triangles and casts; K1 to the end gave 3.4.

**Casts of instances 2 and 3** (-1.0): e9 needs 51.46 us from K2 to K3, the changed kernel 49.78. These 1.7 would be the bound I gave, but they are also what e9's granted clock of 0.83 between 140 and 150 is worth; e2, with these casts on ScalarE and the same 0.83, needs 52.09. Behind K2 the casts' worth is not shown by this pair. e18 against e2 is the better one, 3.1 us by the runs for the middle parts of all instances, with a difference of clock as well.

**GpSimd** (0): nearly right, 0.4 us of waiting, and 1.4 us more when the zeroing is doubled. One took 0.414 us, where I had 0.5. "GpSimd's small loads move to where it is idle: 0" was right for these kernels, and it hid the most expensive dependence of the change: left where they were, the loads cost 4.6 to 7.5 us.

**Order of the rest** (0): not nothing but some -4 us by e2 against e15, the bound I gave. Both have the zeroing, so this holds what the new list does for the triangles' gain: nothing of it is left in the old list (e10), 1.9 us in the new one (e5).

Sum by stretches, in the spans: +7.4 - 2.8 - 1.7 - 0.8 - 0.9 = +1.2, where the forecast had +7.3 - 3.2 - 6.3 = -2.2. The triangles' 3.8 us too much are more than the whole difference of 3.4; that the rest nearly cancels is luck, since the order wasn't nothing and the casts' worth isn't where I had put it.

**The signs.** M1 near 61, the late `q_lo`, the casts gone and no L1334 came out. TensorE's busy time fell by 7.5 us (294.3 to 286.8) and not by 25: most of the triangles' records lay inside those of their neighbours, which busy time counts once. None of the signs of being wrong appeared: VectorE was idle for 3 of 30 us, values waited 0.4 us for GpSimd, and the end was shorter.

**The rivals.** The slower one said that the start's loss decides if the middle gives less than 7.3; the middle and the rest gave 6.2, so its condition was met, at +1.2 to +1.8 and not +7.9. Its mechanism, triangles that become waits of TensorE for a maximum, is what the waits from K1 to K2 show, in the old list more than in the new one. "More in the middle" and "zeroing in the way" didn't happen; the latter is e4's +1.7%, 5.8 us, in a kernel where the loads weren't moved. The rule of the Trainium skill ("SBUF — State Buffer", on the shared port pair), by which VectorE's steps with two SBUF inputs might wait for the zeroing, cost next to nothing. By that section of the Trainium skill the instruction that starts first holds the pair and the other one waits, whichever engine's it is. I had told only half of it; single rows agree with both halves. Where VectorE was first, it wasn't slowed: the subtraction for q's low part at 132.35 took 0.68 with a zeroing from 132.49, and it was the two zeroings that took 1.17 in place of 0.79. Where GpSimd was first, VectorE waited: the `qres` subtraction at 81.92 took 1.01 in place of 0.69 beside `Zimg` from 81.70, and one step of `turn_back` (L1102) at 153.33 took 0.48 in place of 0.29 behind a zeroing from 153.26. The slowed rows of VectorE add up to under 1 us.

## What to carry to other kernels

Before an engine that nobody waited for is put on a path, read everything that its queue issues: bursts of DMA issues that cost nothing before are then in front of the bound. An operation taken off an engine with waits of its own gives back less than its stream, and may give less than its share of the chain too: look at what the engine will wait for once it is gone. And a late start costs only what isn't work that must be done anyway: ask what else stands in the start, and where it would go.

## What had not been expected

- ScalarE is slower at casts that VectorE does: R2 0.72 against 0.42 us, R2T 0.58 against 0.42, for the same 128x512. Together with `Y` (0.80) a tile takes 2.1 us of one engine.
- The ten microseconds with a single wait of 3.1 us on TensorE had a granted clock of 0.56 (e4); where the wait was gone it was 1.00 (e10).
- VectorE relieved of half the length of its 128 full maxima (0.69 to 0.42 us each, 30 us of busy time) shortened the span by 5.0 us only, and the time by 1.15%, 3.9 us.
